# A graph-network kernel on one core: the flags of doubtful lines gathered by a transfer of GpSimd, and one register loaded by VectorE in place of four

## What is computed

```
for n in range(2):
    q = Xa @ W1.T @ W2.T;  k = Xa @ W3.T
    probs = softmax(q @ k.T)
    # of each row, in falling order: keep while the sum so far is under 0.9
    keep = cumsum(sorted probs) - sorted probs < 0.9
    A = probs * keep;  A = A / A.sum(-1)
    Xf = R @ Xf;  Xa = A @ Xa
    Z = Z + Xf @ U1[n].T + Xa @ U2[n].T
```

## Time and profile before

| | us |
|---|---|
| median of 3 runs | 1050.21 (1046.84 to 1052.52) |
| the profiled execution's own time | 1052.0 |
| its span in the profile | 1050.2 |
| TensorE busy | 811.1 (77%) |
| VectorE busy | 778.6 (74%) |
| ScalarE busy | 510.8 (49%) |
| GpSimd busy | 68.0 (6%) |
| chain that ended last | PE 38%, DVE 37%, ACT 11%, issue 9% |

### The profile page before, as it was taken

One profiled execution on the slowest core, in us unless ns is written; L12 is line 12 of the kernel. 1 busy time (PEld: TensorE's weight loads), 2 busy tenths in 40 slices (PEclk: granted clock), 3 DMA queues, 4 the chain that ended last, 5 costly groups with the idle time before them and its releaser, 6 DMA issues.

```text
span 1050.2 us, 12275 instructions
## 1 busy us (share of the span) xinstructions
PE 811.1 (77%) x3886; PEld 556.4 (53%) x3886; DVE 778.6 (74%) x2363; ACT 510.8 (49%) x981; POOL 68.0 (6%) x63
## 2 busy tenths in 40 slices
PE   5889947777887853929678968858668999996795
PEld 5744414545665732728266647647356485553342
DVE  5968778988998998970798899799799512325715
ACT  4877235367468476404552754764865232023112
POOL 0020001000000000000000000020101100003201
PEclk9999977888988985959788779979879999998798
DMA  9949304334004000000044220230351447400001
GB/s 338 351 165 432 137 0 161 120 121 161 1 1 161 1 0 2 1 2 1 1 160 148 97 78 1 96 121 1 105 234 41 159 203 297 183 1 0 1 0 40
DMA packets 20221, 108.25 MB, mean 103 GB/s; under 512 B 1824, under 2 KB 8752, under 8 KB 9776
## 3 DMA queue, kind: packets, MB, share of 16 engines
q1 hardware_dynamic: 18752, 106.77, 27.3%
q10 hardware_dynamic: 1392, 0.61, 0.2%
HBM read 88.23 MB, written 19.14 MB: 102 GB/s over the span
## 4 chain that ended last, share of the span: by engine, by line
PE 38%; DVE 37%; ACT 11%; issue 9%; POOL 2%; DVEq 1%; DMA 1%; POOLq 0%; SPq 0%; ACTq 0%
DVE AT L1500 13%; PE PS L788 8%; PE PS L657 5%; DVE mxv L1639 5%; PE PS L527 4%; PE PS L857 3%; DVE AT L2086 3%; DVE nd L1503 3%; ACT BC L1229 3%; PE PS L1038 3%; PE PS L1014 3%; PE PS L710 3%; ACT AT L1229 2%; PE PS L1044 2%; DVE se L1493 2%
## 5 line engine op out<-in xcount | busy, mean ns | idle before, releaser
L1060 ACT ACTIVATE AT<-PS 128x512 f32<-128x512 f32 (+2 forms) x240 | 119.0, 568 | 118.9 <-PE PS L527 100.7
L527 PE MATMUL PS<-ident,AT 128*128 128x128 f32 x544 | 87.6, 298 | 57.8 <-DVE rS L2141 24.4
L1500 DVE SCALAR_TENSOR_TENSOR AT<-EA,se 128x2048 uint8<-128x2048 f32 (+1 forms) x46 | 107.6, 2345 | 1.5 <-DVE se L1493 0.3
L527 PEld LDWEIGHTS PS<-ident,AT 128*128 128x128 f32 x544 | 70.8, 155 | 66.3 <-DVE rS L2141 26.0
L710 PE MATMUL PS<-K,ST 64*128 64x512 f32 x256 | 91.5, 810 | 17.4 <-ACT EA L1197 10.9
L1500 DVE SCALAR_TENSOR_TENSOR AT<-AT 128x2048 uint8<-128x2048 f32 (+2 forms) x48 | 96.1, 2002 | 2.3 <-PE PS L527 1.3
L2086 DVE MAX8 AT<-AT 128x8 f32<-128x256 f32 x256 | 87.6, 412 | 0.7
L1639 DVE TENSOR_REDUCE mxv<-PS 128x1 f32<-128x2048 f32 x32 | 73.2, 2288 | 15.1 <-PE PS L710 14.7
L788 PE MATMUL PS<-AT 128*128 128x128 f32 x512 | 72.4, 292 | 12.5 <-ACT AT L1060 12.0
L788 PE MATMUL PS<-hr,AT 128*128 128x128 f32 x512 | 72.8, 293 | 8.5 <-ACT AT L1060 7.5
L788 PEld LDWEIGHTS PS<-AT 128*128 128x128 f32 x512 | 65.9, 202 | 21.4 <-ACT AT L1060 17.1
(11 more groups left out here) (293 smaller groups left out, 1458.7 us busy)
## 6 DMA issues: line engine op xcount, KB each, us to landing
AT<-keep_at SPq DMA_DIRECT2D x32, 1024.0 KB, 5.1
EA<-in_adj SPq DMA_DIRECT2D x20, 1024.0 KB, 6.4
keep_at<-AT SPq DMA_DIRECT2D x8, 2048.0 KB, 24.8
AT<-keep_at SPq DMA_DIRECT2D x8, 2048.0 KB, 12.4
AT<-in_adj SPq DMA_DIRECT2D x12, 1024.0 KB, 4.9
EA<-keep_degrees SPq DMA_DIRECT2D x1, 1024.0 KB, 6.5
keep_x<-K SPq DMA_DIRECT2D x4, 256.0 KB, 8.6
out<-EA SPq DMA_DIRECT2D x4, 256.0 KB, 2.3
```

The lines of the kernel that those rows point to most:

```text
L527: return pe.transpose(dst, src, ident[0:p, 0:p])
L1060: return act.activation(dst, src, ACT.Copy)
L1500: return dve.scalar_tensor_tensor(out=o, in0=x0, scalar=s, in1=x1, op0=op0, op1=op1, **k)
```

## The change

Line numbers of the changed kernel are 2 to 14 higher. `doubtful` gets `left`. For `left > 0` it no longer calls `any_row` but raises `doubt_ok`; GpSimd waits for that and issues a transfer of the 128 flags `fl[:, 0:1]` to 128 words of partition 0 (`doubts`). Where VectorE loaded four registers, it waits for `doubt_in`, takes the maximum of the 128 words, and loads one register. If a line is doubtful, `any_row` is made up for in the branch. For `left == 0` (groups 3 and 7) all stays. On GpSimd the power of each group is now ahead of the block with `norm_root(0)`, which is asked for in the pass of group 6, and the transfer of each group stands behind its power.

```diff
@@ gpsimd
             for gi in range(STEPS * NB):
-
-                if gi == STEPS * NB - 1:
+                pool.wait_ge(exp_ok, G * gi + G)
+                if gi > 1:
+                    pool.wait_ge(kept_ok, gi - 1)
+                pool.tensor_tensor(sZ[:, gi % 2, :], Z[:, gi % 2, :], ex[:, 1, 0:G], ALU.pow).then_inc(root_ok, 1)
+                if gi == STEPS * NB - 2:
                     pool.wait_ge(un_z, 2 * UNITS)
                     pool.wait_ge(early_in, 3 * 16)
                     pool.tensor_tensor(WT[:, U1T, :], ident[:, :], early_g, ALU.mult).then_inc(diag_ok, 1)
                     pool.wait_ge(diag_ok, 1)
                     norm_root(0)
-                pool.wait_ge(exp_ok, G * gi + G)
-                if gi > 1:
-                    pool.wait_ge(kept_ok, gi - 1)
-                pool.tensor_tensor(sZ[:, gi % 2, :], Z[:, gi % 2, :], ex[:, 1, 0:G], ALU.pow).then_inc(root_ok, 1)
+                if gi % NB < NB - 1:
+                    pool.wait_ge(doubt_ok, gi - gi // NB + 1)
+                    pool.dma_start(doubts, fl[:, 0:1]).then_inc(doubt_in, 16)
@@ vector: doubtful
-                any_row(v)
+                if left > 0:
+                    dve.sem_inc(doubt_ok, 1)
+                else:
+                    any_row(v)
@@ vector: group
-                load_more()
                 if left > 0:
+                    dve.wait_ge(doubt_in, 16 * (gi - gi // NB + 1))
+                    v(dve.tensor_reduce(any_doubt[:, :], doubts, AX.X, ALU.max))
+                    dve.reg_load(more[0], any_doubt[0:1, 0:1])
                     masked(v, E)
+                else:
+                    load_more()
                 with dve.If(dve.snap(more[0])):
                     if left > 0:
                         v.wait()
+                        m = Dyn(sure_steps, sures, 2)
+                        any_row(m)
+                        m.end()
```

More of the change, by code:

```diff
@@ L153, in gnn_kernel @@
                  for m in range(2)]
+        doubts = row[0:1, 9, 2 * BK + 3 * P:3 * BK].bitcast(I32)
         junks = [row[:, 10, k * BK:(k + 1) * BK].bitcast(U8) for k in range(G)]
@@ L202, in gnn_kernel @@
         ft = sb("ft", [P, 32], I32)
+        any_doubt = sb("any_doubt", [1, 1], I32)
         ones = sb("ones", [P, WINDOW])
@@ L233, in gnn_kernel @@
             sure_steps ksum_ok mean_mm mean_ok lnz_ok gap_ok guess_steps guess_ok
-            cs_ok at_saved un_half un_st un_t un_row un_pr un_z th_ok sum_ok roots_ok fin_sq bias_ok h2_t h2_st hw_mm x2_ok mask_ok
+            cs_ok at_saved un_half un_st un_t un_row un_pr un_z th_ok sum_ok roots_ok fin_sq bias_ok h2_t h2_st hw_mm x2_ok mask_ok doubt_ok doubt_in
             ln_steps ln_sq ln_var ln_pow ln_root ln_y ln_t ln_ts ln_x ln_x2 h2_act diag_ok early_in x2_dma"""
@@ L243, in gnn_kernel @@
          ksum_ok, mean_mm, mean_ok, lnz_ok, gap_ok, guess_steps, guess_ok,
-         cs_ok, at_saved, un_half, un_st, un_t, un_row, un_pr, un_z, th_ok, sum_ok, roots_ok, fin_sq, bias_ok, h2_t, h2_st, hw_mm, x2_ok, mask_ok,
+         cs_ok, at_saved, un_half, un_st, un_t, un_row, un_pr, un_z, th_ok, sum_ok, roots_ok, fin_sq, bias_ok, h2_t, h2_st, hw_mm, x2_ok, mask_ok, doubt_ok, doubt_in,
          ln_steps, ln_sq, ln_var, ln_pow, ln_root, ln_y, ln_t, ln_ts, ln_x, ln_x2, h2_act, diag_ok, early_in, x2_dma) = [sem(n) for n in names.split()]
@@ L2033, in surely, with doubtful @@
                 any_row(w)
-            def doubtful():
+            def doubtful(left):
                 v.wait()
@@ L2104, in group @@
                 crossing_checked(q)
-                doubtful()
+                doubtful(left)
                 if left > 0:
```

## The result

| | before | after |
|---|---|---|
| median (lowest to highest), 15 runs each | 1050.22 us (1044.96 to 1053.87) | 1055.1 us (1051.64 to 1057.67) |
| ratio of the times | | 1.0042, 95% interval 1.0023 to 1.0062 |
| the profiled execution: own time, span | 1052.0, 1050.2 us | 1054.44, 1052.6 us |
| mean granted TensorE clock | 0.877 | 0.874 |

The forecast was 1054.6 us (1048 to 1062). The kernel before was timed again in four later batches, and in one of them the changed kernel too: 1055.19 against 1052.09, a ratio of 1.003 (1.0009 to 1.005). The change costs 3 to 5 us.

The account below looks back on a forecast made before the run. No engine is full; TensorE and VectorE share the chain that ended last, with ScalarE behind. A 9.3 us loss less a 4.9 us gain is 4.4 us more: from 1050.2 to 1054.6 us, range 1048 to 1062.

Parts of the forecast that it names:

- The stand (term 3): Group 6: norm_root(1), queued behind GpSimd's new wait for the flags, leaves ScalarE standing still for 9.3 us.
- Its inner working: GpSimd, group 6: power of group 7 ends 0.9 to 1.0 us after VectorE's pass, then norm_root(1) takes 1.56 us.
- The flags (term 1): VectorE at the flags: transpose and maximum go, 0.42 us less per group, counted once, in group 2.
- The loads (term 2): VectorE ahead of masked: one load for four, 1.15 us less in groups 1, 4, 5, 1.04 in group 2; 4.5 us.
- in groups 1, 4 and 5 VectorE sets the chain from there on: Behind the loads: the 1.15 us saved in each of these groups counts in full.
- group 0 gains nothing: Group 0: ScalarE's last sum ends at 259.75, VectorE reads it at 259.87, so the shorter loads save nothing.
- The transfer (term 4): From flags to maximum: the transfer lands in under 5.6 us, the room in group 2, and costs nothing.
- Rival B: VectorE ahead of masked: the transfer lands late, beyond 5.6 us; 1060.1 us at 10 us, 1070.5 at 12.4; chance 0.13.
- rival C: GpSimd in group 6: issuing the transfer takes longer than VectorE's pass hides; 1057 to 1060 us, taken as 1058; chance 0.15.
- The sum: Whole kernel: 9.3 us lost less 4.9 gained is 4.4 us more, a median of 1054.6 us.
- The gain as forecast by the page: Loads: with the page's floor of about 600 ns, each group gains 0.18 us less, 0.7 in all.

Follow-up runs that it names:

- Run 1: The changed kernel with norm_root(1) moved ahead of GpSimd's wait for group 6's flags; 1046.75 us, ratio 0.9977 to the kernel before.
- run 2: The kernel before with only a wait added: GpSimd's power of group 7 waits for group 6's flags; 1061.45 us, ratio 1.0112.
- Run 5: The changed kernel with GpSimd's power of group 7 moved ahead of group 6's transfer; one profiled execution, ScalarE stood still for 8.14 us.
- Run 3: Run 1's kernel with any_row for every group and the four loads kept, the transfers' result unread; 1050.27 us, ratio 1.0005 to the kernel before.
- run 9: Run 1's kernel again, unchanged, timed in one batch with the changed kernel; 1051.17 us, ratio 0.9977 to the kernel before.
- run 12: Run 1's kernel, with VectorE in the last group also waiting for GpSimd's last norm_root before its four passes; 1046.21 us, ratio 0.9956 to the kernel before.
- run 4: The kernel before with one register load in place of four where groups follow, seeing 32 of 128 partitions' flags; 1048.59 us, ratio 0.9981.
- run 6: The kernel before with its four register loads moved right behind the issue of mass_above's pass, no transfer; 1039.91 us, ratio 0.9915.

## Why the prediction was right, and where a term was off

- **The stand (term 3), 9.3 us: right, in place and size.** ScalarE stood 9.25 us (9.26 in two more profiles), the product behind it came 9.4 us later. Run 1 takes it away, run 2 makes it alone.
- **Its inner working: right.** The power of group 7 was to end 0.9 to 1.0 us behind VectorE's pass. It ended at 749.80, the pass at 748.90. In run 2, where the power began with the pass, it took 3.13 us and ended at 756.22, 0.86 us behind the pass. Run 5 shows that it is the pass that holds GpSimd, not the power's length: there `nd` is held in its place.
- **The flags (term 1): right per group.** The pass began 0.14 us after the reduction's end in group 6 (746.41 to 746.55), where with transpose and maximum it was 0.50 (751.76 to 752.26): 0.36 us in place of 0.42. But the prediction counted it only in group 2. See the next point.
- **The loads (term 2): near their size, but not where they count.** From `negmax` or the copy to the pass it takes 0.74 to 1.00 us in the changed kernel, where 0.85 was assumed. Flags to `kept_ok` per group, before and after, each from one trace; and below it from a group's flags to the next group's, medians of four profiles with VectorE's old code (the kernel before twice, runs 2 and 3) and of seven with the new (the changed kernel three times, runs 1, 5, 9 and 12):

| group | 0 | 1 | 2 | 4 | 5 |
|---|---|---|---|---|---|
| flags to `kept_ok` before, us | 19.96 | 21.86 | 17.47 | 20.43 | 22.88 |
| after, us | 18.60 | 21.40 | 15.97 | 19.45 | 21.60 |
| less | 1.36 | 0.46 | 1.50 | 0.98 | 1.28 |
| flags to the next flags before, us | 77.39 | 78.69 | 65.08 | 76.53 | 80.44 |
| after, us | 75.70 | 78.39 | 63.56 | 76.51 | 80.37 |
| less | 1.7 | 0.3 | 1.5 | 0.0 | 0.1 |
| forecast, with term 1 | 0 | 1.15 | 1.46 | 1.15 | 1.15 |

  5.6 us are gained inside the groups, and some 3.3 arrive at group 6. The step that failed is "in groups 1, 4 and 5 VectorE sets the chain from there on": there next to nothing arrives. VectorE comes sooner and waits. Behind groups 1 and 4 the way to the next flags is 57.0 to 57.1 us in nearly all of the seven, with 0.6 to 0.7 us of waits for TensorE's transposes (L531) and ScalarE's `gs`, against 56.5 without them in seven of eight cases before; behind group 5 VectorE waits 2.2 us for ScalarE's `gs` in five of the seven, 0.6 in two of the four before. I checked the meetings with ScalarE's sums and not these. The other way round, "group 0 gains nothing" was wrong too: it gives the most.
- **The transfer (term 4): nothing, right.** It lands in 2.0 to 3.2 us; VectorE nowhere waits for `doubt_in`. Rival B needed 5.6 us, rival C an issue of more than 2.3 us on GpSimd, and that took 0.60 to 0.75. Run 3 puts both together at 0.05% (-0.15 to 0.26).
- **The sum: right partly by luck.** 9.4 less 3.3 would be 6.1 us; measured were 4.4 (2.4 to 6.5) and 3.2 (0.9 to 5.3). So a gain too large by 1.6 us brought the forecast to 4.4, and something that the prediction did not have brought the measured times below 6.1. A likely part of it is time that the kernel before loses by itself in some executions: its first profile takes 4.1 us more than the second ahead of group 6's flags and 2.3 more behind them, and its 15 times spread over 9 us, those of the changed one over 6. This is argued, not shown. Whether the collision of the last group has a part in it I have not seen, since both profiles of the kernel before show GpSimd ahead; I leave it open. (In the chances, 0.21, 0.13 and 0.15 make 0.49, not 0.47; nothing hangs on it.)
- **What the prediction did not have** is that collision. It did not touch the changed kernel, whose three profiles have GpSimd 0.6 to 0.7 us ahead of the passes. It would explain why run 1 and run 4 fell short of 4.9 and 5.6 us: run 12 takes it away and gets 4.6 us (2.6 to 6.6), of which its profile shows the 3.3 of the groups, or somewhat more, and 0.9 that the last group itself gained, since GpSimd was not held there at all (20.96 us from its flags to TensorE's last eight products L862, 21.90 in the first profile of run 1's kernel). That the heap above 1051 us is made of such executions is shown for one of them by its trace, and for the rest argued from run 12.

On the pages that the prediction weighed: the Trainium skill (DMA: Bandwidth & Descriptors, section "Latency and other measured facts") gives a register load from memory a floor of about 600 ns. No load here took that long: 297 to 561 ns in the traces of the kernel before, the changed one and run 1. The gain as forecast by the page, an estimate of 4.2 us, would have been nearer to the 3.3 that arrived, but for another reason, and the time worked out from it, 5.1 us more, farther from the 4.4 measured.

The Trainium skill (SBUF — State Buffer, section "SBUF: two separate sides") shuts out GpSimd's writing of descriptors while VectorE runs an operation in a two-port mode, and the prediction asked what would follow if VectorE's pass did so. All six transfers were issued beside a `mass_above` pass of VectorE, in 0.60 to 0.75 us each: no run shows that lock-out. The same section has another rule for an operation of VectorE with two inputs in SBUF: it locks the port that VectorE and GpSimd share only against an operation of GpSimd that reads SBUF, and whichever starts first keeps it to its end. That is what the traces show: beside these passes the transfers are free and GpSimd's arithmetic is held, and `es`, begun 0.31 us ahead of the passes in the last group of the changed kernel (829.21, with the passes from 829.52), took its usual 1.01 us.

## What to carry to other kernels

Before you shorten a wait, ask whether it can be hidden where it is: four loads under a running pass cost nothing (9 to 12 us gained, of which the traces place 7.4 to 8.1), while one load in place of four cost a transfer, a wait on another engine, and what was queued behind that wait. A wait that is put into an engine's program delays all that stands behind it there: find the last instruction behind it that another engine needs, and put that one ahead. And when an engine becomes faster, look at what it now runs beside; a wait that keeps two engines out of each other's way cost nothing in run 12 and may pay for itself.

## What the runs showed of the hardware

- A small operation of GpSimd that comes while VectorE makes a pass over 128x2048 with two inputs in SBUF is held until that pass is over. The power of 128x4 takes 1.01 us alone and took 1.9 to 3.1 us where it came into such a pass, in all 14 traces ending 0.86 to 0.90 us behind it; `nd`, 0.19 us alone, ended 0.05 to 0.06 us behind the pass and took up to 1.78 us in the last group. Beside VectorE's MAX8 operations, which have one input, the power took its 1.01 us (649.90 in the kernel before), and so did `es` where it had begun ahead of the pass. Where four passes follow each other directly, `es` took 3.00 us in place of 1.01: it was let in at the border between two passes, not at the end of the four.
- A transfer of 128 words from 128 partitions to one, issued by GpSimd, takes it 0.60 to 0.75 us even beside such a pass, and lands in 1.9 to 3.4 us over the eight traces that have it.
- Register loads go on beside a running pass of their own engine; four of them, 0.3 to 0.55 us each, left no idle time behind the 2.35 us pass in run 6.
- In run 9 TensorE waited 3.3 us longer ahead of 24 products than in run 1, and these took 13.46 us in place of 10.54, the granted clock of the stretch at 0.78 in place of 1.00. In run 4 a gap of 3.47 us was followed by 12.03 us, at 0.88. All are single executions, and no run shows that the gap is the cause: ahead of an earlier eight products of the same line stands a gap of 2.48 us in several profiles, and they took 5.37 us behind it in the kernel before (811.27) and 3.67 in the changed one (815.98).
